# An attention kernel on one core: values gathered by index on GpSimd, two fewer units turned on TensorE, and another order of the prologue

## The reference

```python
x = x + einsum('bsi,boi->bso', x, weight[ids])                  # L0
q, k, v = x @ Wq.T, x @ Wk.T, x @ Wv.T                          # per head, D = 128
q, k = rope(rmsnorm(q, q_norm_w)), rope(rmsnorm(k, k_norm_w))
kc, vc = k_cache[block_table], v_cache[block_table]             # 512 cached keys a batch
scores = q @ concat(kc, k) / sqrt(D); masked where key >= length
o = softmax(scores) @ concat(vc, v)
x = x + o @ Wo.T
```

## Time and profile before

| what | us |
|---|---|
| median of the runs | 1006.95 |
| profiled execution, span | 1006.6 |
| TensorE busy | 994.3 (99%) |
| VectorE busy | 861.5 |
| ScalarE busy | 810.3 |
| GpSimd busy | 795.8 |

### The profile page before, as it was taken

The page is one execution under the profiler, slowest core; times in us unless marked ns, Lnnn a source line. Parts: engine busy times, 40 slices in busy tenths (PEclk is TensorE's granted clock), DMA queues, the critical chain, the costliest instruction groups (busy, mean ns, idle before and its releaser), DMA issues.

```text
span 1006.6 us, 19441 instructions
## 1 busy us (share of the span) xinstructions
PE 994.3 (99%) x5471; PEld 864.3 (86%) x5471; DVE 861.5 (86%) x1787; ACT 810.3 (80%) x2109; POOL 795.8 (79%) x811
## 2 busy tenths in 40 slices
PE   8999999999999999999999999999999999999998
PEld 6778888888888888888888888888888888888886
DVE  7676657799999899999998999899999999998995
ACT  4455456698889889888988898898888988988884
POOL 4876677497889879897898888898798978888672
PEclk9999999999999999999999999999999999999999
DMA  8999879899988888888988888888988879888873
GB/s 254 277 262 260 283 229 258 213 211 201 221 162 162 161 158 153 166 157 152 171 153 162 156 160 165 148 168 155 170 148 165 157 151 166 162 162 144 153 149 84
DMA packets 513643, 180.94 MB, mean 180 GB/s; under 512 B 429873, under 2 KB 495682, under 8 KB 513538
## 3 DMA queue, kind: packets, MB, share of 16 engines
q1 hardware_dynamic: 381280, 143.20, 68.9%
q10 hardware_dynamic: 131106, 34.15, 15.3%
q0 software_dynamic: 1152, 2.36, 0.8%
HBM read 105.45 MB, written 31.86 MB: 136 GB/s over the span
## 4 chain that ended last, share of the span: by engine, by line
PE 95%; DVE 2%; ACTq 1%; issue 1%; ACT 1%; another core or an unknown queue 0%; POOL 0%; DVEq 0%
PE S L1408 22%; PE O L1341 7%; PE O L1343 7%; PE O L1342 7%; PE Q L1341 6%; PE Q L1343 6%; PE Y L1341 6%; PE Q L1342 6%; PE Y L1343 6%; PE Y L1342 6%; PE T L1347 4%; PE KV L1342 3%; PE KV L1341 3%; PE KV L1343 3%; PE KV L1361 1%; PE Y L1361 1%
## 5 line engine op out<-in xcount | busy, mean ns | idle before, releaser
L1080 DVE SCALAR_TENSOR_TENSOR pr<-pr,rc,raw 128x640 f16<-128x640 f32 x220 | 258.8, 1177 | 15.3 <-ACT raw L817 8.3
L1052 DVE CUSTOM_DVE_ANT_0 pr<-S,mask,rst 128x640 f32<-128x640 f32 x256 | 225.4, 881 | 16.6 <-PE S L1408 13.3
L837 ACT ACTIVATE pr<-pr,nb 128x640 f32<-128x640 f32 x256 | 211.7, 827 | 14.5 <-DVE nb L1052 14.5
L817 ACT ACTIVATE raw<-pr,rc 128x640 f16<-128x640 f32 x220 | 176.2, 826 | 0.6 <-DVE rc L1068 0.4
L617 POOL TENSOR_TENSOR m<-m 128x512 f32<-128x512 f32 x63 | 112.5, 1786 | 73.7 <-DVE m L1119 69.8
L591 POOL TENSOR_SCALAR ptl<-first 128x512 fp32r<-128x512 f16 x140 | 111.8, 799 | 17.6 <-issue 6.0
L570 POOL TENSOR_TENSOR kl<-raw,kh 128x512 fp32r<-128x512 f32 x64 | 97.8, 1528 | 34.5 <-ACT kh L720 33.5
L1408 PE MATMUL S<-kh,qh 128*128 128x320 f32 x512 | 120.8, 317 | 3.7 <-DVE nb L1052 3.6
L591 POOL TENSOR_SCALAR ptl<-turned 128x512 fp32r<-128x512 f16 x135 | 108.3, 802 | 11.2
L1408 PE MATMUL S<-kh,ql 128*128 128x320 f32 x512 | 116.8, 309 | 0.0
L783 ACT ACTIVATE Q<-Q 128x128 f32<-128x128 f32 x256 | 68.2, 266 | 59.9 <-DVE m L1119 59.9
(11 more groups left out here) (179 smaller groups left out, 2674.9 us busy)
## 6 DMA issues: line engine op xcount, KB each, us to landing
wraw<-in_wall SPq DMA_DIRECT2D x74, 256.0 KB, 4.4
cache_rows<-in_kv ACTq DMA_DIRECT2D x80, 224.0 KB
raw<-cache_rows SPq DMA_DIRECT2D x57, 256.0 KB, 4.0
raw<-cache_rows ACTq DMA_DIRECT2D x53, 256.0 KB, 5.0
mask<-mask_rows SPq DMA_DIRECT2D x64, 128.0 KB
cache_rows<-in_kv SPq DMA_DIRECT2D x36, 224.0 KB
first<-in_lw SPq DMA_DIRECT2D x5, 1024.0 KB
cache_rows<-in_kv SPq DMA_DIRECT2D x16, 192.0 KB, 4.2
```

What stands on the lines that cost most here:

```text
L817: e.activation(upper16[:, g, :], pr[:, slot(u, g), :], ACT.Copy, scale=rc[:, u % 2, g:g + 1]).then_inc(a_f1, 1)
L837: e.activation(pr[:, slot(u, g), :], pr[:, slot(u, g), :], ACT.Exp, bias=nb[:, u % 2, g:g + 1], scale=-1.0, accum_out=sm[:, u % 2, g:g + 1 ...
L1052: e.tensor_tensor_reduce(pr[:, slot(u, g), :].rearrange("p (a n) -> p a n", a=2), S[:, :, 0:320], mask[:, u % 2, :].rearrange("p (a n) -> ...
L1080: e.scalar_tensor_tensor(out=lower16(u, g), in0=pr[:, slot(u, g), :], scalar=rc[:, u % 2, g:g + 1], in1=upper16[:, g, :], op0=ALU.mult, op ...
```

## The change

Values: all 64 units' values are now gathered by GpSimd, one indirect DMA a unit. The value cache is laid out with four tokens a row (VK = 4, 2 KB), so 128 rows are a unit's 512 values; row numbers for all units are made on VectorE (`value_rows`). The keys' columns are permuted in the same way: the key cache is laid out by page, dimension, token in four, row, and the high and low splits of keys read it through `by_tile` and write through `tiles_of` (runs of 8 floats). The copies to the DRAM buffer hold keys alone (8 or 7 rows a page in place of 14 or 12) and `load_v` is gone.

Units: NA is 6 in place of 8 and NL is NA + 1, so two units fewer are turned on TensorE, and the copy tables are new.

GpSimd's second loop has `values_hi` and `values_lo` ahead of `q_sum`, and the gather of unit i after the scales, waiting for VectorE's lower planes of unit i - 1. Here is GpSimd's list for one period whose weight split comes first and the start of the next such one, before; wl, kl, m, vh, var, rst, vl and ptl are the tiles written.

```diff
-NL = NB + 1
-NA = 8
+NA = 6
+NL = NA + 1
...
-COPY_SP = (0, 1, 1, 1, 1, 1, 1, 2, 0, 1, 1, 1, 1, 1)
-COPY_ACT = (2, 2, 3, 2, 2, 3, 3, 2, 1, 0, 0, 0, 0, 0)
+COPY_SP = (0, 1, 1, 1, 1, 1, 1, 2, 2, 2, 2, 1)
+COPY_ACT = (2, 3, 3, 3, 3, 3, 0, 0, 0, 0, 0, 0)
...
+            def gather_v(v):
+                e.wait_ge(c_kidx, v // NB + 1)
+                if v >= 2:
+                    e.wait_ge(g_vlo, v - 1 if v <= NA else v)
                 e.indirect_dma_start(
+                    out=rawv[raw_at(v)].rearrange("p t d -> p (t d)"), out_offset=None, in_=vc,
+                    in_offset=bass.IndirectOffsetOnAxis(ap=kidx[:, v:v + 1], axis=0)
                 ).then_inc(d_rawv[v % 2], 16)
...
-                minus(kl[:, j % 2, 0:512], rawk[raw_at(j)], kh[:, j % 2, 0:512]).then_inc(g_kc, 1)
+                minus(tiles_of(kl[:, j % 2, 0:512]), by_tile(rawk[raw_at(j)]),
+                      tiles_of(kh[:, j % 2, 0:512])).then_inc(g_kc, 1)
...
                 split_w(i, 0)
                 if nxt:
                     keys_lo(j)
+                values_hi(w)
+                values_lo(w)
+                if nxt:
                     q_sum(j)
-                values_hi(w)
                 if nxt:
                     scales(j)
-                values_lo(w)
+                if i < NU:
+                    e.wait_ge(v_f2, G * (w - NA) + G)
+                    gather_v(i)
                 if w < LAST:
                     for t in range(3):
                         p_lo(w, t)
...
             e.activation(warmed[:, :], mhalf[:, :], ACT.Sin)
-            e.wait_ge(d_page, 16)
-            load_kt(e, copy_regs[0:4], 0, 3)
+            split_chunk(0, 0)
             e.wait_ge(c_ang, ANG_SIN)
             e.activation(sn, ang, ACT.Sin).then_inc(c_sin, 1)
+            l0_hi(0)
+            split_chunk(0, 1)
             e.wait_ge(c_ang, ANG_COS)
             e.activation(cs, rnd, ACT.Sin).then_inc(c_cos, 1)
-            split_chunk(0, 0)
-            split_chunk(0, 1)
-            l0_hi(0)
             for c in range(2, 6):
                 split_chunk(0, c)
...
+                if i == 0:
+                    k_sum(j)
                 if i >= 0:
                     largest(i, 2)
                 if turn:
                     p_lo(w, 2)
-                k_sum(j)
+                if i != 0:
+                    k_sum(j)
```

More of the change, by code:

```diff
@@ L24 @@
 PSZ = 32
+VK = 4
+ROWS = PSZ // VK
 KEYS = 640
@@ L97, in copies_of, with build @@
             for k in range(first, first + (COPY_ACT if act else COPY_SP)[period])]
-def build(nc, x, xt, lw, wall, kv, ids_lens, table, pages, qkw, consts, iota, out):
+def build(nc, x, xt, lw, wall, kc, vc, ids_lens, table, pages, qkw, consts, iota, out):
     with ExitStack() as ctx:
@@ L408, in load_x @@
                 if b == 0:
-                    for t in range(4):
+                    for t in range(2):
                         e.dma_start(ws[:, t, :],
@@ L500, in _ @@
             load_mask(1)
-            load_kt(e, kt_regs, 1, 1)
             load_x(2)
-            for t in range(2, NT):
+            for t in range(1, NT):
                 load_kt(e, kt_regs, 1, t)
@@ L843, in _ @@
             e.dma_start(cst[:, :], consts).then_inc(d_ids, 16)
+            e.dma_start(tabb[:, :], table).then_inc(d_tab, 16)
+            e.wait_ge(d_page, 16)
+            e.load(id_reg_act, page[0:1, NB * NPG:NB * NPG + 1])
+            number = e.snap(id_reg_act, min_val=0, max_val=15)
+            for t in range(2, 4):
+                e.dma_start(lws[:, t, :], lw[bass.ds(number, 1), t * P:(t + 1) * P, :].rearrange(
+                    "a p n -> (a p) n")).then_inc(d_lw[0][t], 16)
             e.dma_start(qkw_s, bc(qkw, 2 * D)).then_inc(d_small, 16)
-            for g in range(4):
-                e.dma_start(tabb[32 * g:32 * g + 32, :],
-                            table[g:g + 1, :].broadcast_to([32, NB * NT])).then_inc(d_tab, 16)
             for c in range(6):
@@ L1193, in _ @@
             e.tensor_scalar(ang, ang, PI_IN, -PI_IN, ALU.min, ALU.max).then_inc(c_ang, 1)
+            table_rows()
+            value_rows(0)
+            l0_add(0)
+            split_chunk(0, 0)
+            l0_lo(0)
+            split_chunk(0, 1)
             e.wait_ge(c_ang, ANG_SIN)
@@ L1213, in _ @@
                 turn = w >= 0
-                if i == 2:
-                    key_rows_1()
+                for hk in range(2 * i - 1, 2 * i + 1):
+                    if 1 <= hk < NK:
+                        value_rows(hk)
                 if o >= 0:
@@ L1365, in l0_product @@
             def l0_product(b):
-                for t in range(4):
+                for t in (0, 2, 1, 3) if b == 0 else range(4):
                     l0_part(b, t)
```

177 lines of the change are left out of this document (63 added, 114 removed).

## The result

The changed kernel takes 1029.05 us (median of 4 runs, 1028.45 to 1029.63); the old one, run beside it on the same chip, 1005.58 (1002.95 to 1007.05). The ratio is 1.024, 95% interval 1.0218 to 1.0261. The profiled execution has a span of 1026.6 us, 20.0 more than before.

The account below looks back on a forecast made before the run. TensorE, never idle in the middle, was taken as the bound, with GpSimd 1.01 us from delaying it. Span 1006.6 - 4.4 + 29.2 + 0 = 1031.4, at the median 1031.8, so 1032 us; range 1003 to 1049.

Parts of the forecast that it names:

- The bound and the place: TensorE never stops in the middle; it would wait at the turn of m behind GpSimd's m, some 27 times by about 1 us.
- (c): GpSimd's `values_hi` and `values_lo` ahead of `q_sum`: 1.08 us stall in each of 27 heavy periods, +29.2 us, bounds +13 to +46.
- (b): One values gather a unit on GpSimd, standing where vl stood: 1.25 us of GpSimd's time, nothing added to the sum.
- Rival C: Gather late or held up: landing 10.5 us after issue would cost 25 us on top, 1057 us; chance 0.11.
- The forecast's other doubt: VectorE's lower plane or `k_sum` could hold up the new gather on GpSimd: one lock, 0.6 to 0.8 us, which p_lo can spare.
- (a): Units 6 and 7 not turned on TensorE: 40 transposes fewer, -4.4 us; their DMAs beside the copies 0, bounds -1 to +3.
- (d): Prologue: new waits and gains at the first units sum near 0; taken as 0, bounds -2 to +3 us.
- the wait at the third tile: First unit's `project_q`: TensorE waits 2.1 us for the third weight tile, since ScalarE's chunk work stands behind angles and cos.
- The clock that the new wait could lose: Prologue: the new 2.1 us wait in `project_q` can lower TensorE's granted clock, +1 to +1.7 us.
- The gain at 41 us: Period 0: `k_sum` ahead of the third `largest` shortens TensorE's 1.23 us wait, giving back 0.7 us, and 1 to 1.7 of clock.
- (e): Key splits on permuted columns, read in runs of 8 floats: 0, bounds 0 to 0.6 us on kl in a heavy period.
- Rival B: No wait at the turn: kl ends before 503.5 in heavy periods, vh and vl fit in, 1002.5 us; chance 0.24 with half-way cases.

Follow-up runs that it names:

- experiment 4: Changed kernel without the gathers of the second loop (units 7 to 63 compute with stale values): 1024.05 us, ratio 1.0176.
- experiment 3: Old kernel with only `values_hi` and `values_lo` moved ahead of `q_sum` and the scales, values still loaded by SP: 1026.21 us, ratio 1.0208.
- Experiment 6: Changed kernel with GpSimd's old order in heavy periods only, the gather there behind the third p_lo: 1030.74 us, ratio 1.0275.
- experiment 5: Old kernel with NA = 6 and adapted copy tables, full-size copies of keys and values kept: 1015.74 us, ratio 1.0102.
- Experiment 8: Changed kernel with the last two angle steps ahead of the first layer-0 sum on VectorE, cos ahead of `l0_hi(0)` on ScalarE: 1031.19 us, ratio 1.0263.
- experiment 7: Old kernel with the values ahead of `q_sum` and, on VectorE, the second `largest` ahead of the fourth lower plane: 1067.71 us, ratio 1.0631.
- experiment 11: Old kernel with only the change's place for unit 1's `k_sum` (VectorE) and key turn (TensorE): 1005.31 us beside 1004.51, ratio 1.0005.
- experiment 12: Changed kernel with the first two units' key pages back on both queues and the mask's rows written earlier: 1027.77 us, ratio 1.0232.
- experiment 1: Changed kernel with GpSimd's old order (`q_sum`, `values_hi`, scales, `values_lo`) in the second loop, then the gather: 1100.96 us, ratio 1.0941.
- experiment 10: Changed kernel with GpSimd's old order in all periods and the gather behind the third p_lo: 1035.03 us, ratio 1.0306.

## Why the prediction was right, and where its terms were not

**The bound and the place** held. The forecast had TensorE waiting at the turn of m behind GpSimd's m, about 27 times; it waits 26 times, in the heavy periods and nowhere else in the middle. vh and vl stand ahead of m and take 0.62 and 1.75; m takes 1.28, free of the lock, as the step said, but it is vl and not vh that is held, by 0.45 us and not 0.6. The heavy periods cost 15.1 to 15.4 us, the light ones 14.5; only one of eight, a light one, is 14.8 to 15.0.

**(c) was mis-sized**: 18.2 us for +29.2, or 21.0 with the gathers. The forecast took kl's end at 4.33 us into every heavy period and so m's at 8.40 and a stall of 1.08. In the first heavy period of a pair this nearly holds: kl ends at 4.49, m at 8.14, and the turn is 0.88 late. In the second, kl ends at 4.18 and m at 7.85, and the turn is 0.58 late: nothing is inherited, since TensorE's wait moves the next `project_q` back as well, and GpSimd's p_lo, behind a gather and not a two-input vl, are a little quicker (0.76 us for 0.80 on the mean; why is open, since in experiment 4 they have neither ahead of them and take 0.81). The mechanism the forecast had from the earlier trace rows, two-input work on the two engines shutting each other out, is shown on both sides; the Trainium skill's "SBUF — State Buffer", section "SBUF: two separate sides", calls it an exclusive lock where the first to start keeps it, and the trace agrees with 1.76 and 1.42 us for 1.07 and 0.87. The forecast followed the lock only from VectorE to GpSimd, and did not ask what vh and vl do to VectorE: that is a second limit, at `scores`, which costs 18 to 20 us by itself when kl is early (experiments 3 and 4). The step had the turn of m as the only one.

**(b) was too cheap.** GpSimd's 1.25 us held, at 0.96 to 1.17, and the gather landed in time: 4.8 us at the median for 256 KB, as the DMA view says, where the old kernel's of 64 KB took 4.7:

```profile
raw<-in_vc,kidx POOLq DMA_INDIRECT x64, 4.8
```

Rival C is refuted for this kernel: no vh waits for its gather. Experiment 6, with the gather 3 p_lo later, is where it begins to hold. The forecast's other doubt, the gather beside a lower plane, came to nothing as well: of the 55 planes that start within a gather between 130 and 980 us none takes over 0.89 us. The section "SBUF: two separate sides" of the Trainium skill's "SBUF — State Buffer", which the forecast names for it, ties that warning to VectorE's two-port modes, a condition that the forecast left out. But the gather in vl's place is not free: experiment 4 puts it at 2.8 us in the middle, 1.0 in the tail and 5.0 by the medians. With it GpSimd is busy 271 of 300 us.

**(a)** held: -4.4, and -4.2 and -4.3 between units 6 and 9; the transposes of pr are 40 fewer (132 for 172). That its DMAs cost nothing beside the copies rests on the halved copies (experiment 5).

**(d) failed, past its own bounds**: 0 with -2 and +3, and 3.9 on the mean. `project_q` starts at 14.0 to 15.2 (15.2 to 15.3 before; 14.9 forecast) and the wait at the third tile, forecast as 2.1, is there (17.54, where 15.49 was due). The steps behind it were mis-sized. The turn of the first key was put at 25.1 and the first scores 1.1 late; the turn is at 26.2 on the mean and waits 2.2 us in most traces, because the key's scale now comes with the queries' and these come late, and the first scores are 3.0 late, the first `largest` 3.9. Experiment 8 shows that both hang on the angle steps. The clock that the new wait could lose is lost, 1.7 us. The gain at 41 us that was to balance all this isn't there. Its clock, 0.83 over 40 to 50 us, was one execution's: the old prologue of experiments 3, 5, 7 and 11 has 1.00 there. And TensorE waits 1.16 and 1.69 us. The first comes of a move that I counted as taken from ScalarE's queue and did not add to SP's (experiment 12); the other stands in the old prologue too, where one trace had shown it under another name. Experiment 11 shows that moving `k_sum` is worth nothing.

**(e)** held: kh takes 0.63 us as before, kl 1.30 or 1.88.

**The sum** came within 3 us by luck, because errors of both signs met: (c) 11 too high; (b) 3, (d) 4 and the tail 1 too low. The place and the cause of the wait are not luck. Rival B is refuted too: it needed kl to end before 503.5 - 500.29 = 3.2 us of a heavy period, and it ends at 4.2 to 4.5. More than that, in experiments 3 and 4 kl does end before 3.2 in most heavy periods, and the kernel still loses 18 to 20 us, at `scores`: B's condition would not have saved it. What stays open are 1.6 us between the parts and the medians, less than the prologue moves from one execution to the next.

## What to carry to other kernels

Before moving work ahead of a step with slack, split the periods by what else they hold: GpSimd's mean idle time of 15% was worthless, since the heavy periods had none. And ask of each pair of neighbours on GpSimd and VectorE which gets blocked: gathering work that shares the lock on one made the other late, by 0.4 to 0.7 us an instruction in most places here, and another order only changed the place of the loss or made it larger (experiments 1, 3, 6, 7 and 10; none removed it). Where a load changes queues, add it to the one as well as taking it from the other; and price a prologue, its waits and its clock, from several traces.

## What was unexpected of the hardware

GpSimd's one-input work is shut out as well: vh takes 0.62 us where it has the lock (675.21) and 1.20 where a lower plane started first (642.16, 658.27). The forecast's steps had the lock between two-input work alone; the Trainium skill's "SBUF — State Buffer", section "SBUF: two separate sides", asks for two inputs only on VectorE's side, and the trace agrees. A gather of 128 rows costs GpSimd about as much for rows of 512 B as for 2 KB: 0.94 to 1.22 us, mean 1.01, in the old kernel; 0.96 to 1.17, mean 1.12, in the changed one. An issue that waits for the instruction just ahead of it on the same engine costs 0.81 us of idle time on GpSimd (645.49), so its place matters more than its length: the middle is 89.3 us longer in experiment 1 and 24.1 in experiment 10. And a lower plane that starts within a gather usually takes its 0.9 us, but 29 in experiments 6 and 10, with a wl right behind the gather, took 2.7 to 2.8; why these and not the others, no run here shows.
